# The second norm's rows in the remainder buffer of a fused attention and feed-forward kernel, with new instruction orders

## The chip, the cores and the metric

The kernel runs on one NeuronCore of a Trainium2 chip. The metric is the device time of one execution in microseconds: 1593.41 us, the median of three (1593.0 to 1603.3). The engines are TensorE (PE in the profile, its weight loads PEld), VectorE (DVE), ScalarE (ACT), GpSimd (POOL) and SyncE (SP), which issues the transfers. Each runs its own list of instructions in order; semaphores join them.

## The reference

One pre-norm block over 16 batches of 1024 rows with 256 features, all in float32:

```
xn  = layernorm(x)
Q, K, V = xn @ Wq.T + bq, xn @ Wk.T + bk, xn @ Wv.T + bv
s   = (Q @ K.T) / sqrt(256) * mask          # a Gaussian over the keys
x1  = x + softmax(s) @ V @ Wo.T + bo
x2n = layernorm(x1)
h   = gelu(x2n @ bin(w1).T + b1)            # 1024 hidden, erf gelu
out = x1 + h @ bin(w2).T + b2               # bin(w) = mean(|w|) per row * sign(w)
```

## The kernel before, in words

Every number that enters a matmul is split in two: a high part rounded to the matmul's format (names with h) and a remainder (names with l). Products take high by high, high by remainder and remainder by high. The query and key weights are folded into one matrix M, the value and output weights into one matrix N, so a batch needs *queries* (M times the normalized rows), score tiles against masked keys, a *weighing* of the normalized rows by the exponentials (weigh_rows), and a *projection* by N (project). Signs of w1 and w2 multiply in the feed-forward part; their mean sizes enter as scales.

B = 16 batches, T = 8 tiles of 128 rows, two halves of TH = 4 tiles, C = 2 chunks of 128 features, J = 8 tiles of 128 hidden features, which are computed in J hidden pairs (two tiles of hidden features for 512 rows; pairs 0 to 3 are the first half of the rows).

The order of work on each engine is written out by hand in one function batch(b, more) per engine (TensorE from L1138, VectorE from L845, ScalarE from L607, GpSimd from L431, SyncE's loop at L332). While batch b runs its second part, batch b+1 is prepared: its rows are turned and split, its queries and masked keys made, its score tiles 0 to 3 computed among the hidden pairs and output rows of b, and batch b+2's first norm is taken. TensorE's order in a steady batch b:

- score tiles 4 to 7 of b, each followed by six of the 24 steps of weigh_rows(b, 0);
- queries(b+1); project(b, 0); steps 0 to 15 of weigh_rows(b, 1);
- turn_rows_ffn(b, 0), the **first turn**: eight transposes of the second norm's rows, tiles 0 to 3;
- steps 16 to 23; hidden_pair 0; project(b, 1); hidden_pairs 1 to 3; score tile 0 of b+1;
- turn_rows_ffn(b, 1), the **second turn**, tiles 4 to 7; score tile 1;
- hidden_pairs 4 to 7; output rows 0, 1 (ffn_row); score tile 2; row 2; score tile 3; rows 3 to 7.

How the second norm's rows arise: project leaves its result in PSUM; VectorE adds it to x (add_attention, L743) and takes the statistics; GpSimd computes the root and the negated mean by pairs of tiles (root_ffn, L395 to L400); ScalarE normalizes (normalize_ffn, L519) into xn2(t); TensorE turns four tiles; ScalarE copies the high part (hi_rows_ffn, L524) and VectorE the remainder (lo_rows_ffn, L753) into rows_h and rows_l. xn2(t) lies in the last row slot of the probability buffer. The masked keys of batch b+1 lie there too (rows_t), until ScalarE has copied their high part (hi_keys, L486) and GpSimd has subtracted it (split_keys, L374). So normalize_ffn waits at tiles 0 and 4:

```
if q % TH == 0 and b < B - 1:
    act.wait_ge(kl_set, N2 * (b + 1) + q // TH + 1)
```

In the same stretch GpSimd's order is lo_probs(b, 7), root_ffn 0 and 1, both split_keys(b+1), root_attention(b+2) (L387, L389: the roots of the first norm two batches on), root_ffn 2 and 3. VectorE's is the last transpose of probabilities (turn_probs, L726), the fourth of lo_queries, invert_sums(b, 0) (L736, which waits for the sums that TensorE turns inside project(b, 0)), add_attention of four tiles, the statistics of batch b+2, lo_rows_ffn(b, 0), center_attention(b+2) (L685: waits for root_attention(b+2)), lo_outputs(b, 1) (L731: the remainder of the weighed rows; project(b, 1) needs it from its fifth matmul on), invert_sums(b, 1), add_attention of four tiles, then the splits of the gelu results (split_pair, a cast at L760 and a subtraction at L762). None of this order of GpSimd is changed in a steady batch's stretch, nor that of VectorE from add_attention(0) to split_pair 2.

regrouped_rows is a buffer that holds the first norm's rows of the next batch after a transfer between partitions. rows_l, the remainders, occupies the same memory (a placement without owner), half for half: the transposed rows of b+1 are read from it, and then their remainders are written into it. The queries of b+1 are their last reader.

Exponentials (ScalarE, L501) go to one of three slots of g; SyncE moves them in four transfers between partitions (regroup_probs, L300); VectorE transposes blocks (turn_probs), ScalarE copies the high part (hi_probs, L507), GpSimd the remainder (lo_probs, L382). Tile 7 has slot 3 of the probability buffer (p_slot), since its own is the last row that the masked keys use; its transfer waits for pv_summed, the end of the first weighing.

## Time and profile before

| | |
|---|---|
| runs | 1593.0, 1593.41, 1603.3 us |
| profiled execution | 1601.16 us, span 1599.4 us |
| mean granted clock of TensorE | 0.976 |
| TensorE busy | 1472.0 us, 92% |
| VectorE busy | 1049.8 us, 66% |
| ScalarE busy | 878.9 us, 55% |
| GpSimd busy | 975.6 us, 61% |
| chain that ended last, by engine | PE 33%, DVE 16%, ACT 15%, DMA 12%, POOL 11%, SyncE's queue 7%, issue 5% |

The span runs from the first to the last instruction. Busy shares are means over all stages; what a stage waits for is seen in the waits and timelines. "PE ps L1023 <- ACT probs L519" reads: TensorE's instruction of line 1023, which writes ps, waited for ScalarE's of line 519, which wrote probs. A timeline row gives start, duration, engine, line, what is written from what, the count of merged instructions and, in brackets, the idle time before it and what ended it. Ends of matmuls are modelled.

### The profile page before, as it was taken

To read this page: it belongs to the slowest core of one execution; us is meant where nothing else is said; L and a number is where in the kernel's file an instruction comes from. 1 tells how busy PE (TensorE), PEld (TensorE's weight loads), DVE (VectorE), ACT (ScalarE), POOL (GpSimd) and SP (SyncE) were. 2 spreads that over 40 slices of the span, in tenths; PEclk is the share of its full clock that TensorE was granted. 3 is DMA by queue.
4 is the path that set the end of the run, shared out by engine and by line. 5 is a ranking of instruction groups with operands and counts; after the bars stand their busy time and mean duration, and the time that the engine had idled before them with its cause. 6 is when DMAs were issued, how large, how long until landed. Compare 5 with 4: busy or idle time off the path is not lost.

```text
span 1599.4 us, 21090 instructions
## 1 busy us (share of the span) xinstructions
PE 1472.0 (92%) x7709; PEld 1245.5 (78%) x7709; DVE 1049.8 (66%) x1576; ACT 878.9 (55%) x1238; POOL 975.6 (61%) x1033
## 2 busy tenths in 40 slices
PE   6899999899998999999899998999999999998996
PEld 4678778787787878778787787878778777787876
DVE  7766676666776667666566766666766666764544
ACT  4655564555646455564555655556564555645432
POOL 3656747656675766647566476566747666475543
PEclk9899999999999999999999999999999999999999
DMA  5625516264270735516245261633606355260421
GB/s 185 112 66 78 134 22 122 68 95 117 44 164 4 118 93 79 132 20 115 78 82 130 37 132 44 106 105 61 151 1 119 93 79 133 32 128 26 72 61 27
DMA packets 107939, 138.50 MB, mean 87 GB/s; under 512 B 11822, under 2 KB 95164, under 8 KB 107836
## 3 DMA queue, kind: packets, MB, share of 16 engines
q1 hardware_dynamic: 107808, 137.15, 41.5%
q8 instruction: 61, 1.00, 0.3%
q14 instruction: 42, 0.34, 0.1%
q10 hardware_dynamic: 28, 0.01, 0.0%
HBM read 37.49 MB, written 16.78 MB: 34 GB/s over the span
## 4 chain that ended last, share of the span: by engine, by line
PE 33%; DVE 16%; ACT 15%; DMA 12%; POOL 11%; SPq 7%; issue 5%; ACTq 0%; DVEq 0%; POOLq 0%
PE ps L980 11%; DMA probs<-g 10%; PE ps L1044 8%; PE ps L954 7%; SPq L300 6%; ACT g L542 4%; DVE probs L726 4%; POOL rstd L397 3%; ACT probs L519 3%; POOL kl L374 3%; ACT g L501 3%; POOL probs L382 2%; POOL nmr L400 2%; DVE xin L743 2%; DVE st L747 2%
## 5 line engine op out<-in xcount | busy, mean ns | idle before, releaser
L382 POOL TENSOR_TENSOR probs<-probs 128x512 fp32r<-128x512 f32 x256 | 341.3, 1355 | 191.9 <-ACT probs L507 191.9
L980 PE MATMUL ps<-probs,xnh 128*128 128x512 f32 x1024 | 299.7, 409 | 6.2 <-ACT probs L507 6.1
L1057 PE MATMUL ps<-sgn,probs 128*128 128x256 f32 x1024 | 249.8, 284 | 11.3 <-DVE ys L770 9.7
L1058 PE MATMUL ps<-sgn,probs 128*128 128x256 f32 x1024 | 248.1, 283 | 0.0
L726 DVE STREAM_TRANSPOSE probs<-probs 128x1024 f32<-128x1024 f32 x128 | 159.2, 1243 | 134.5 <-DMA probs<-g 134.2
L507 ACT ACTIVATE probs<-probs 128x1024 fp32r<-128x1024 f32 x128 | 135.6, 1059 | 201.5 <-DVE probs L726 201.2
L980 PEld LDWEIGHTS ps<-probs,xnh 128*128 128x128 f32 x1024 | 200.3, 199 | 51.4 <-issue 9.1
L542 ACT ACTIVATE g<-ps,cols,alpha 128x512 f32<-128x512 f32 x256 | 183.1, 772 | 87.9 <-PE ps L1044 87.9
L1044 PE MATMUL ps<-rows_h,sgn 128*128 128x512 f32 x512 | 202.6, 396 | 26.5 <-DVE rows_l L753 26.5
L420 POOL TENSOR_TENSOR xin<-xin,ys 128x256 f32<-128x256 f32 x128 | 93.9, 738 | 191.7 <-DVE ys L770 191.7
L1057 PEld LDWEIGHTS ps<-sgn,probs 128*128 128x128 f32 x1024 | 195.8, 191 | 18.2 <-DVE ys L770 13.0
L1044 PE MATMUL ps<-rows_l,sgn 128*128 128x512 f32 x512 | 200.9, 392 | 0.0
L501 ACT ACTIVATE g<-ps,nmax 128x1024 f32<-128x1024 f32 x128 | 141.9, 1110 | 100.4 <-DVE nmax L718 99.8
L1058 PEld LDWEIGHTS ps<-sgn,probs 128*128 128x128 f32 x1024 | 196.1, 192 | 1.2
L718 DVE TENSOR_REDUCE nmax<-ps 128x1 f32<-128x1024 f32 x128 | 154.6, 1217 | 64.7 <-PE ps L954 64.4
L954 PE MATMUL ps<-kh,qh 128*128 128x512 f32 x512 | 164.0, 402 | 10.9 <-ACT g L501 4.8
L762 DVE TENSOR_TENSOR probs<-g,probs 128x1024 fp32r<-128x1024 f32 x128 | 163.2, 1275 | 4.4
L519 ACT ACTIVATE probs<-xin,nmr,rstd 128x256 f32<-128x256 f32 x128 | 68.4, 592 | 166.1 <-POOL nmr L400 93.6
L954 PE MATMUL ps<-kl,qh 128*128 128x512 f32 x512 | 159.6, 393 | 0.0
L980 PE MATMUL ps<-probs,xnl 128*128 128x512 f32 x512 | 158.9, 392 | 0.0
L954 PE MATMUL ps<-kh,ql 128*128 128x512 f32 x512 | 158.8, 391 | 0.0
L1044 PEld LDWEIGHTS ps<-rows_h,sgn 128*128 128x128 f32 x512 | 96.6, 189 | 56.0 <-DVE rows_l L753 33.2
(114 smaller groups left out, 2644.4 us busy)
## 6 DMA issues: line engine op xcount, KB each, us to landing
probs<-g SPq DMA_DIRECT2D x512, 128.0 KB, 3.5
xrow<-in_L_attn_x_dram SPq DMA_DIRECT2D x32, 512.0 KB, 8.3
xin<-in_L_attn_x_dram SPq DMA_DIRECT2D x32, 512.0 KB, 8.7
out_dram<-xin SPq DMA_DIRECT2D x31, 512.0 KB, 4.7
regrouped_rows<-xn SPq DMA_DIRECT2D x120, 128.0 KB, 4.6
...
```

The source lines that it names most:

```text
L382: pool.tensor_tensor(ptl(q)[:, half(n)], pt(q)[:, half(n)], pth(q)[:, half(n)].bitcast(F32), ALU.subtract).then_inc(ptl_set, 1)
L501: act.activation(exps(q).rearrange("p (i j r) -> p j i r", j=T, r=QUAD), slot(q % 2).rearrange("p h (j i r) -> p (h j) i r", j=TH, r=QUAD) ...
L507: act.activation(pth(q), pt(q), ACT.Copy).then_inc(pth_set, 1)
L542: last = act.activation(g[:, k % G_SLOTS, half(m)], ps[:, PAIR_BANK[k] + m, :], ACT.Gelu, bias=cols[:, j:j + 1], scale=alpha1[:, j:j + 1])
L718: dve.tensor_reduce(nmax[:, q:q + 1], slot(q % 2), mybir.AxisListType.XY, ALU.max, negate=True).then_inc(max_set, 1)
L726: dve.transpose(pt(q).rearrange("p (j g c) -> p g j c", j=T, c=QUAD), regrouped(q).rearrange("p (g j r) -> p g j r", j=T, r=QUAD)).then_in ...
L762: dve.tensor_tensor(hidden_part(1, n, js), val, hidden_part(0, n, js).bitcast(F32), ALU.subtract).then_inc(gl_set, 1)
L954: last = pe.matmul(ps[:, 2 * (q % 2) + n, :], part[:, c, tile(q)], keys[:, n, c, :], start=c == 0 and part is qh and keys is kh, stop=c == ...
L980: last = pe.matmul(ps[:, PV_BANK + c, :], xv[:, j, tile(c)], probs[:, lo, first:first + TH, tile(j)], start=k == 0, stop=k == len(parts) - 1)
L1044: last = pe.matmul(ps[:, PAIR_BANK[k] + m, :], sgn1[:, c, tile(j)], part[:, n, c, :], start=c == 0 and part is rows_h, stop=c == C - 1 and ...
L1057: pe.matmul(bank, probs[:, 0, r, tile(j)], sgn2[:, j, :], start=j == 0, stop=False)
L1058: last = pe.matmul(bank, probs[:, 1, r, tile(j)], sgn2[:, j, :], start=False, stop=j == J - 1)
```

## The change

The change has these parts.

1. **Second norm's rows.** xn2(t) lies in the second half of regrouped_rows; both halves of the rows use it in turn. normalize_ffn waits at tile 0 for the queries of b+1 (for the last batch, for the hidden pairs of the one before), at tile 4 for the first turn, and no longer for kl_set.
2. **ScalarE's order.** hi_keys(b+1, 1) goes behind hi_rows_ffn(b, 0); hi_outputs(b, 1) goes before the load of gelu's table; gelu pair 2 goes ahead of normalize_ffn(6, 7); hi_rows_ffn(b, 1) ahead of two pieces of hi_values; exponentials(b+1, 3) ahead of hi_probs(b+1, 1) and of the second half of normalize_attention(b+2).
3. **TensorE's order.** The second turn precedes both score tiles 0 and 1 of b+1; output rows 0 to 2 precede score tiles 2 and 3.
4. **VectorE's order.** row_max of score tile 0 precedes lo_rows_ffn(b, 1), that of tile 1 follows split_pair 3; row_max 7 precedes mask_keys(b+1, 1); invert_sums(b, 0) precedes turn_probs(b, 7); scale_outputs 0 precedes split_pair 7, scale_outputs 2 precedes row_max 2, scale_outputs 4 precedes turn_probs 2. GpSimd's lo_probs of b+1 follow output rows 2, 4 and 6.
5. **Last batch.** Tile 7 has its own slot, and its transfer waits for the batch's own kl_set; score tiles in pairs ahead of the weighing; output rows 0 and 1 in banks 0 and 1 before hidden_pairs 4 to 7.
6. **Setup.** w1 and w2 are loaded behind the rows of batch 1 and lie elsewhere; GpSimd makes the signs of w2 in three passes, VectorE only those of w1; score tiles 1 to 5 of batch 0 come before most of the turned signs; ScalarE takes exponentials 0, 1 and 2 of batch 0, with two tiles of normalize_attention(1) after each of the latter, the copy of tile 0, exponential 3, turned signs, the copy of tile 1, two more pairs of normalized tiles around exponential 4, and so comes to the copy of tile 3 and exponential 5; the eight mean sizes of w1, the turned signs of w2 and the spread of alpha2 move into batch 0, before and behind exponentials 6 and 7.

Its core (the placement of w1s, w2s and diag, the arguments b in p_slot's callers and what only moves in the setup of ScalarE and VectorE are left out; the moves above name them):

```diff
+        def p_slot(b, q):
+
+            return TH - 1 if q == T - 1 and b < B - 1 else q
+
...
         def xn2(t):
-            return probs32[:, t // TH, LAST_ROW, (t % TH) * D:(t % TH + 1) * D]
+            return regrouped_rows[:, 1, (t % TH) * D:(t % TH + 1) * D]
...
             for n in range(N2):
                 load_rows(1, n)
+            sp.dma_start(w1s[:], w1.rearrange("(j p) d -> p j d", p=P)).then_inc(w1_loaded, 16)
+            sp.dma_start(w2s[:], w2.rearrange("(c p) h -> p c h", p=P)).then_inc(w2_loaded, 16)
             sp.dma_start(bias_bc[:], bo.partition_broadcast(P)).then_inc(bcast_loaded, 16)
             sp.dma_start(b2_bc[:], b2.partition_broadcast(P)).then_inc(bcast_loaded, 16)
 
             def regroup_probs(b, q):
                 sp.wait_ge(exp_set, T * b + q + 1)
-                if q == T - 1:
+                if q == T - 1 and b < B - 1:
                     sp.wait_ge(pv_summed, N2 * b + 1)
+                elif q == T - 1:
+                    sp.wait_ge(kl_set, N2 * (b + 1))
+                if b == 0 and q == 5:
+                    sp.wait_ge(signs2_set, 1)
                 elif b > 0:
                     sp.wait_ge(ffn_summed, T * (b - 1) + q + 1)
                 for i in range(QUADS):
-                    sp.dma_start(regrouped(q)[i * QUAD:(i + 1) * QUAD, :],
+                    sp.dma_start(regrouped(b, q)[i * QUAD:(i + 1) * QUAD, :],
                                  exps(q)[:, i * (S // QUADS):(i + 1) * (S // QUADS)]).then_inc(p_back[q % QUEUED], 16)
 
...
                 regroup_rows(1, n)
+                regroup_probs(0, TH + n)
             for b in range(B):
-                for q in range(TH, T):
+                for q in range(TH if b > 0 else TH + N2, T):
                     regroup_probs(b, q)
...
+            root_attention(1)
             lo_values(0)
-            root_attention(1)
+            pool.wait_ge(w2_loaded, 16)
+            pool.tensor_scalar(sw2[:], w2s[:], 0.0, None, ALU.is_gt).then_inc(pos2_set, 1)
+            pool.wait_ge(alphas_set, C)
+            pool.wait_ge(pos2_set, 1)
+            pool.tensor_scalar(w2s[:], w2s[:], 0.0, None, ALU.is_lt).then_inc(neg2_set, 1)
+            pool.wait_ge(neg2_set, 1)
+            pool.tensor_tensor(sw2[:], sw2[:], w2s[:], ALU.subtract).then_inc(signs2_set, 1)
             lo_probs(0, 0)
             lo_probs(0, 1)
             lo_probs(0, 2)
-                    if more and r in (2, 3, 5):
-                        lo_probs(b + 1, (2, 3, 5).index(r))
+                    if more and r in (2, 4, 6):
+                        lo_probs(b + 1, r // 2 - 1)
...
-                    if q % TH == 0 and b < B - 1:
-                        act.wait_ge(kl_set, N2 * (b + 1) + q // TH + 1)
+                    if q == 0 and b < B - 1:
+                        act.wait_ge(q_summed, QG * (b + 2))
+                    elif q == 0:
+                        act.wait_ge(hidden, J * b)
+                    if q == TH:
+                        act.wait_ge(x2_turned, N2 * b + 1)
                     act.wait_ge(nmr2_set, T * b + q + 1)
                     act.activation(xn2(q), xin[s][:, q, :], ACT.Identity, bias=nmr2[:, q:q + 1],
                                    scale=rstd2[:, q:q + 1]).then_inc(xn2_set, 1)
...
@@ -633,21 +656,22 @@
                 hi_probs(b, 7)
                 if more:
                     hi_keys(b + 1, 0)
-                    hi_keys(b + 1, 1)
                 normalize_ffn(b, range(0, 4))
                 hi_rows_ffn(b, 0)
+                if more:
+                    hi_keys(b + 1, 1)
+                hi_outputs(b, 1)
                 load_table(b, ACT.Gelu)
-                hi_outputs(b, 1)
                 gelu_pairs(b, range(0, 1))
                 if more:
                     hi_values(b + 1, range(0, 2))
                 normalize_ffn(b, range(4, 6))
-                gelu_pairs(b, range(1, 2))
+                gelu_pairs(b, range(1, 3))
                 normalize_ffn(b, range(6, 8))
-                gelu_pairs(b, range(2, 4))
+                gelu_pairs(b, range(3, 4))
+                hi_rows_ffn(b, 1)
                 if more:
                     hi_values(b + 1, range(2, QG))
-                hi_rows_ffn(b, 1)
                 gelu_pairs(b, range(4, J))
                 if not more:
                     return
@@ -657,11 +681,11 @@
                 if b + 2 < B:
                     normalize_attention(b + 2, tiles_of(0))
                 exponentials(b + 1, 2)
+                hi_probs(b + 1, 0)
+                exponentials(b + 1, 3)
+                hi_probs(b + 1, 1)
                 if b + 2 < B:
                     normalize_attention(b + 2, tiles_of(1))
-                hi_probs(b + 1, 0)
...
                 turn_probs(b, 5)
+                row_max(b, 7)
                 if more:
                     mask_keys(b + 1, 1)
-                row_max(b, 7)
+                if b == 0:
+                    dve.wait_ge(alpha2_spread, 1)
+                    dve.tensor_copy(alpha2_bc[:], ps[:, QO_BANK, 0:D]).then_inc(alpha2_set, 1)
                 turn_probs(b, 6)
                 lo_outputs(b, 0)
                 if more:
                     lo_queries(b + 1, range(0, 3))
+                invert_sums(b, 0)
                 turn_probs(b, 7)
                 if more:
                     lo_queries(b + 1, range(3, QG))
-                invert_sums(b, 0)
                 for q in tiles_of(0):
                     add_attention(b, q)
...
@@ -883,27 +905,33 @@
                 split_pair(b, 0)
                 split_pair(b, 1)
                 split_pair(b, 2)
+                if not more:
+                    split_pair(b, 3)
+                    lo_rows_ffn(b, 1)
+                    scale_outputs(b, 0, more)
+                    scale_outputs(b, 1, more)
+                    for k in range(4, J):
+                        split_pair(b, k)
+                    for r in range(2, T):
+                        scale_outputs(b, r, more)
+                    return
+                row_max(b + 1, 0)
                 lo_rows_ffn(b, 1)
                 split_pair(b, 3)
-                if more:
-                    row_max(b + 1, 0)
-                    row_max(b + 1, 1)
-                for k in range(4, J):
+                row_max(b + 1, 1)
+                for k in range(4, J - 1):
                     split_pair(b, k)
-                if not more:
-                    for r in range(T):
-                        scale_outputs(b, r, more)
-                    return
                 scale_outputs(b, 0, more)
+                split_pair(b, J - 1)
                 scale_outputs(b, 1, more)
+                scale_outputs(b, 2, more)
                 row_max(b + 1, 2)
-                scale_outputs(b, 2, more)
                 turn_probs(b + 1, 0)
                 row_max(b + 1, 3)
                 turn_probs(b + 1, 1)
                 scale_outputs(b, 3, more)
+                scale_outputs(b, 4, more)
                 turn_probs(b + 1, 2)
-                scale_outputs(b, 4, more)
                 scale_outputs(b, 5, more)
                 scale_outputs(b, 6, more)
                 turn_probs(b + 1, 3)
...
             def ffn_row(b, r, more):
-                bank = ps[:, QO_BANK + r % 2 if more else PV_BANK + r % 2, 0:D]
+                bank = ps[:, (QO_BANK if more else 0) + r % 2, 0:D]
                 if r == 0:
-                    pe.wait_ge(gelu_set, J * (b + 1) - (1 if more else 0))
+                    pe.wait_ge(gelu_set, J * (b + 1) - 1 if more else J * b + 2)
                 if r % TH == 0:
                     pe.wait_ge(gl_set, J * b + (J // N2) * (r // TH + 1))
...
+            scores(0, 1)
+            scores(0, 2)
             turn_signs1(range(0, 2))
-            scores(0, 1)
             pe.wait_ge(bvb_set, C)
             for e in range(C):
                 last = pe.matmul(ps[:, 6, 0:D], bvb[:, e, :], woT[:, e, :], start=e == 0, stop=e == C - 1)
             last.then_inc(bias_summed, 1)
+            scores(0, 3)
+            scores(0, 4)
+            scores(0, 5)
             turn_signs1(range(2, 2 * C))
-            scores(0, 2)
-            pe.wait_ge(diag_set, C)
-            pe.wait_ge(nl_set, 1)
-            for c in range(C):
-                last = pe.matmul(ps[:, 7, c * P:(c + 1) * P], ones[:], diag[:, c, :], start=True, stop=True)
-            last.then_inc(alpha2_spread, 1)
-            scores(0, 3)
+
...
             def batch(b, more):
-                scores(b, TH)
                 if b == 0:
+                    weigh_rows(b, 0, range(0, 6))
                     turn_signs2(range(0, 2))
-                    scores(b, TH + 1)
+                    scores(b, 6)
+                    weigh_rows(b, 0, range(6, 12))
+                    scores(b, 7)
+                    weigh_rows(b, 0, range(12, 18))
                     turn_signs2(range(2, 4))
-                for i in range(TH):
-                    if i > (1 if b == 0 else 0):
+                    weigh_rows(b, 0, range(18, 24))
+                    spread_alpha2()
+                elif more:
+                    for i in range(TH):
                         scores(b, TH + i)
-                    weigh_rows(b, 0, range(6 * i, 6 * i + 6))
+                        weigh_rows(b, 0, range(6 * i, 6 * i + 6))
+                else:
+                    scores(b, 4)
+                    scores(b, 5)
+                    weigh_rows(b, 0, range(0, 6))
+                    scores(b, 6)
+                    scores(b, 7)
+                    weigh_rows(b, 0, range(6, 24))
                 if more:
                     queries(b + 1)
                 project(b, 0, more)
...
                 hidden_pair(b, 1)
                 hidden_pair(b, 2)
                 hidden_pair(b, 3)
-                if more:
-                    scores(b + 1, 0)
+                if not more:
+                    turn_rows_ffn(b, 1, more)
+                    for r in range(0, 2):
+                        ffn_row(b, r, more)
+                    for k in range(4, J):
+                        hidden_pair(b, k)
+                    for r in range(2, T):
+                        ffn_row(b, r, more)
+                    return
                 turn_rows_ffn(b, 1, more)
-                if more:
-                    scores(b + 1, 1)
+                scores(b + 1, 0)
+                scores(b + 1, 1)
                 for k in range(4, J):
                     hidden_pair(b, k)
-                if not more:
-                    for r in range(T):
-                        ffn_row(b, r, more)
-                    return
-                ffn_row(b, 0, more)
-                ffn_row(b, 1, more)
+                for r in range(0, 3):
+                    ffn_row(b, r, more)
                 scores(b + 1, 2)
-                ffn_row(b, 2, more)
                 scores(b + 1, 3)
                 for r in range(3, T):
                     ffn_row(b, r, more)
```

## Rows read from the trace of the kernel before

**Rows 1.** The page, busy time: us, share of the span, instructions.

```profile
PE 1472.0 (92%) x7709; PEld 1245.5 (78%) x7709; DVE 1049.8 (66%) x1576; ACT 878.9 (55%) x1238; POOL 975.6 (61%) x1033
```

**Rows 2.** Waits of TensorE: us in total, times, longest.

```profile
PE ps L1023 <- ACT probs L519: 47.6, 17, 3.1
...
PE ps L1044 <- DVE rows_l L753: 26.5, 16, 3.6
...
PE ps L1057 <- DVE ys L770: 9.7, 15, 0.9
...
PE ps L980 <- ACT probs L507: 6.1, 9, 2.0
...
PE ps L954 <- ACT g L501: 4.8, 15, 0.3
```

**Rows 3.** Timeline of TensorE, first turns: start us, us, [idle before].

```profile
99.63 1.09 PE L1023 MATMUL ps<-ident,probs 128*128 128x128 f32 x8 [2.79 <-ACT probs L519]
...
387.44 1.97 PE L1023 MATMUL ps<-ident,probs 128*128 128x128 f32 x8 [3.09 <-ACT probs L519]
...
1449.68 1.97 PE L1023 MATMUL ps<-ident,probs 128*128 128x128 f32 x8 [3.10 <-ACT probs L519]
```

**Rows 4.** Timeline of TensorE, one steady batch.

```profile
292.72 1.09 PE L1023 MATMUL ps<-ident,probs 128*128 128x128 f32 x8 [2.78 <-ACT probs L519]
...
299.37 0.40 PE L1003 MATMUL ps<-Nl,probs 128*128 128x256 f32 x2
...
299.86 0.50 PE L1003 MATMUL ps<-Nh,probs 128*128 128x256 f32 x2
...
307.82 0.39 PE L1044 MATMUL ps<-rows_l,sgn 128*128 128x512 f32 x1
...
310.89 1.09 PE L1023 MATMUL ps<-ident,probs 128*128 128x128 f32 x8
...
316.77 0.50 PE L1044 MATMUL ps<-rows_h,sgn 128*128 128x512 f32 x1 [1.54 <-DVE rows_l L753]
```

**Rows 5.** One stretch: length, busy time by engine, granted clock, DMA.

```profile
579.00:585.00 6.00, 5.96 (x25) 5.21 (x26) 1.30 (x2) 2.51 (x3) 2.49 (x3) 0.75 0.01 3
```

**Rows 6.** Timeline of GpSimd, the same batch.

```profile
287.66 5.71 POOL L374 TENSOR_TENSOR kl<-probs,kh 128x1024 fp32r<-128x1024 f32 x2
...
293.61 1.65 POOL L389 TENSOR_TENSOR rstd<-ve,mhalf 128x8 f32<-128x8 f32 x1
...
308.45 1.49 POOL L400 TENSOR_SCALAR nmr<-mv,rstd 128x1 f32<-128x1 f32 x2
```

**Rows 7.** Timeline of VectorE, the same batch.

```profile
279.63 1.24 DVE L726 STREAM_TRANSPOSE probs<-probs 128x1024 f32<-128x1024 f32 x1
...
296.05 0.16 DVE L685 SCALAR_TENSOR_TENSOR nmr<-mv,rstd 128x8 f32<-128x8 f32 x1
...
298.58 1.23 DVE L731 TENSOR_TENSOR probs<-ps,probs 128x1024 fp32r<-128x1024 f32 x1 [2.38 <-ACT probs L511]
...
308.35 1.23 DVE L762 TENSOR_TENSOR probs<-g,probs 128x1024 fp32r<-128x1024 f32 x1
```

**Rows 8.** Timeline of ScalarE, the same batch.

```profile
281.86 3.92 ACT L486 ACTIVATE kh<-probs 128x1024 fp32r<-128x1024 f32 x2
...
293.85 1.03 ACT L524 ACTIVATE rows_h<-ps 128x1024 fp32r<-128x1024 f32 x1 [1.18 <-PE ps L1023]
...
309.74 1.09 ACT L519 ACTIVATE probs<-xin,nmr,rstd 128x256 f32<-128x256 f32 x2 [2.15 <-POOL nmr L400]
```

**Rows 9.** Timeline of TensorE, in the setup and in the last batch.

```profile
57.15 1.97 PE L1134 MATMUL ps<-ident,sw 128*128 128x128 f32 x8 [6.33 <-DVE sw L777]
...
1537.09 0.70 PE L980 MATMUL ps<-probs,xnh 128*128 128x512 f32 x2 [1.96 <-ACT probs L507]
...
1568.96 0.79 PE L1044 MATMUL ps<-rows_h,sgn 128*128 128x512 f32 x1 [3.65 <-DVE rows_l L753]
```

194 lines of the change are left out of this document (101 added, 93 removed).

## The prediction

> **What bounds the kernel now.** I read the busy times first, then the waits of TensorE, then its timeline through one steady batch, then the other engines there. TensorE is busy for 92% of the span [rows 1], so only its gaps can be won. The list of its waits names them [rows 2]: 47.6 us before the turn of the second norm's rows (L1023), 16 long waits of about 2.98 us each; 26.5 us before a hidden pair (L1044), which is 1.53 us in each of 15 batches and 3.65 in the last; 9.7 us before the output rows (L1057), 6.1 us before the weighing of rows (L980) and 4.8 us before a score tile (L954).
>
> I count a batch from the start of the first turn, A. The 15 starts from 99.63 to 1449.68 are 96.43 us apart in the mean [rows 3]. From 292.72 to 387.44 it is 94.72 [rows 3, 4]. The difference is mostly the clock: after the idle 2.78 us at 292.72 eight transposes take 1.09 us, after 3.09 us at 387.44 they take 1.97; in such a stretch the granted clock was 0.75 of full, a mean over time at 2.4 GHz and at 1.2 GHz [rows 5]. The first turns that came after 3.09 and 3.10 us lost clock at once; after 2.78 and 2.79 they began at full speed [rows 3, 4]. I put the loss at 1.4 us per batch of the 1.7; the rest is scatter of small waits.
>
> **The first turn.** ScalarE writes the normalized rows into rows that the masked keys of the next batch still occupy, so it waits for both key splits of GpSimd, 5.71 us from 287.66 to 293.37 (the first suffices for the first half) [rows 6]. The rows then go to the remainder buffer, free since the queries. What is late next is the last negated mean of the first half: GpSimd ends the two small groups at 287.7, where its key split starts. invert_sums now precedes the last transpose of probabilities. That one stood at 279.63 [rows 7], before the sums were turned; it would start about 0.9 us later. Hence the copy of tile 7 is late by as much, the weighing of the second half gains a stall of about 0.5 us, and the negated means end at 288.6. The last tile, normalized by 289.2, still precedes TensorE's arrival at 290.4 (292.72 less 2.78, and 0.5): the whole wait and its clock loss go. Bounds for the new stall: 0 and 0.9.
>
> **What is put behind it.** hi_keys(b+1, 1) now comes after hi_rows_ffn(b, 0) on ScalarE, but GpSimd's queue is unchanged: second key split, then root_attention(b+2); and VectorE's queue is unchanged: lo_rows_ffn, center_attention(b+2), which waits for that root, then lo_outputs(b, 1), for which project(b, 1) waits. Before, the whole chain was over at 296.05 [rows 7]. Now it starts from A:
> - the copy of the turned rows starts 1.13 us after A and takes 1.03 [rows 4, 8];
> - one key copy, half of 3.92: 1.96 [rows 8];
> - one key split, half of 5.71: 2.86, and the root, which ends at 295.26, 1.89 us after the splits [rows 6];
> - centering, to the start of the next, 0.1; lo_outputs 1.23 [rows 7];
> - some 0.2 for the hand-offs. Sum: 10.4 us.
>
> At present the matmul that needs lo_outputs starts at 299.86, 7.14 after A, and TensorE had run out 7.05 after A (299.37 and 0.40) [rows 4]. So TensorE stands for about 3.4 us, 3.3 of them new, in the middle of project(b, 1), in the 14 batches that have a batch after the next. That is longer than the idle times after which the clock fell at once.
>
> **The second turn.** Its rows depend on a chain that starts at that same matmul: additions, statistics, roots, normalization. It ends 299.86 to 310.83, 10.97 us (309.74 and 1.09), and the turn started at 310.89 [rows 4, 8]. Now no score tile covers it: hidden_pair 3 ends at 308.21 (307.82 and 0.39), so the turn waits 2.7 us. VectorE's third gelu split now begins while GpSimd computes the last negated mean; I add 0.15 us. In exchange rows_l comes under 5.45 us of score tiles: copy after gelu 3, lo_rows_ffn after row_max, ready 6.2 us after the turn's start, needed at 6.3. The wait of 1.5 goes, just. The clock loss that follows the 3.4 us falls on matmuls before the turn. Where it delays the sums it delays the chain (about 1.0 us), where it delays only hidden pairs the 2.7 us absorb it. For a second loss after the second turn I take 0.2.
>
> **Sum for one of 14 batches.** From A to hidden_pair 4: before 24.05 (292.72 to 316.77) and 1.4 of clock, 25.45. After: 10.4 + 11.15 + 1.2 + 6.35 (transposes 0.9, two score tiles 5.45) = 29.1. That is +3.65. From there to the next A: -2.98 and 0.1 of restart; -0.4, since three output rows now precede the score tile that waits for exponentials [rows 2]; -0.4 of the 9.7/15 = 0.65 before output rows, since scale_outputs(4) goes ahead of a transpose; -0.3 before the first weighing (6.1 less 1.96, over 15), since exponentials(3) is ahead of a copy; +0.5 of above. That is -3.6 to -3.7. Net: -0.05, or -0.7 us in 14 batches. A large gain and a large cost cancel.
>
> **Batch 14** has no root or centering behind the keys: 7.14 + 11.15 + 0.2 + 6.35 = 24.85 against 25.45, and -1.1 of small waits: -1.7.
>
> **The last batch.** Two score tiles go ahead, and tile 7 has a slot of its own, so its transfer need not wait for the first weighing: the wait of 1.96 at 1537.09 goes [rows 9] with about 1.4 of clock: -3.4. At the end, 3.65 us before hidden_pair 4 [rows 9] and, since gelu has the time of two rows more, 1.5 before the first output row go; new is a wait of 2.4 us before output row 0, for gelu 3 and its split. With clock I take -4.0 (bounds -6 and -1).
>
> **The setup.** The longest wait, 6.33 us at 57.15 for w2's signs [rows 9], goes: GpSimd makes them (three passes over 2048 elements) beside scores. I followed the new order: five score tiles in a row, then the weighing waits some 5 us for the copy of tile 3, the tile whose exponential stands behind the normalization; later the turned signs wait for ScalarE after eight mean sizes. The loads of w1 and w2 go behind the next rows on SyncE's queue, and should land before their use. I take -2.5 (bounds -9 and +4: no row shows these passes on GpSimd; the nearest, a key split of 1024 elements, bounds each by 2.9 and 5.7). The first A saves its 2.79 against 0.5 of stall: -2.3.
>
> **Total:** -0.7 - 1.7 - 3.4 - 4.0 - 2.5 - 2.3 = -14.6 us. The profiled execution took 1601.2 us, 1.8 more than its span, and would take 1586.6. It lies 7.8 above the median of the runs, 1593.4; taken from that it gives **1579 us**.
>
> **Rivals.**
> 1. The centering chain is hidden. Without 3.3 us and its 1.0 of clock, 14 batches give 60 us more: 1519. For it: nothing in the rows; it would need GpSimd to finish 3 us earlier than its queue allows. 8%.
> 2. The clock is kept through the 3.4 us. Then 1.0 to 1.2 less per batch, 15 us: 1564. For it: the turn after 2.78 us kept it [rows 4]; against it: those after 3.09 and 3.10 did not [rows 3]. 17%.
> 3. Slower: the last negated mean collides with the third split. The second of two such operations ended at 309.94, when VectorE's second split was over (309.58) [rows 6, 7]. Gelu 2 is now moved ahead, so VectorE's next cast starts there. If the small operation, 0.25 us alone, is held through a cast and a subtraction, it comes 1.0 us later (1.49 for a pair instead of 0.50 is what such neighbours cost before). The second turn's wait then passes 3.1 us, and it loses clock after it as well: 1.4. That is 2.4 us in 14 batches, +34: 1613. It decides from a second-turn wait of 3.1 us. Against it: the small operations do slip in between two VectorE operations, each time. 14%.
> 4. The change doesn't do what it says, because another reader holds the buffer: queries(b+1) are its last, and these end before the first projection, and the first turn comes another two thirds of a weighing later. The wait would stay: about 1%.
>
> For the third, the trace shows a pair of small GpSimd operations at 1.49 us beside VectorE's subtraction [rows 6]. The Trainium skill, "SBUF — State Buffer", section "Who interferes with whom", says that a VectorE instruction with two SBUF inputs, or a cast in a two-port mode, holds the shared port pair for its whole length and that whoever issues first keeps it. By that rule the forecast holds if the small operation wins the gap between two instructions, and the third rival's 1613 us if it loses twice.
>
> **How the numbers follow.** Forecast 60%, own range 1568 to 1592 (setup 6, last batch 3, and 0.8 us per batch either way). With the second rival the low side is 1555; the high side, up to where the third begins, is 1605. About 2 in 10 lie outside. About 1% (16 us) is what a measurement of this kernel can tell from no change. Faster than 1577.5: a little under half of the forecast (0.28), rivals 1 and 2 (0.25), less a share of the second: 0.48. Within 1%: 0.38. Slower than 1609: 0.14, the third.
>
> **What will show it.** L1023 falls out of the first place of TensorE's waits for the first turn, but stays with 2.7 to 2.9 us for the second. L1044 before hidden_pair 4 vanishes. A new wait appears at the project's fifth matmul for lo_outputs of 3.3 us in 14 batches, with VectorE idle at centering until the root of GpSimd. The granted clock falls right behind it. The forecast is wrong if that wait is missing, or if the second turn waits over 3.1 us, or if the first turn still waits.

## The result, and the profile after

The changed kernel takes 1610.4 us (median of 14 runs, 1608.8 to 1617.9); the kernel before, beside it, 1601.0 (14 runs, 1593.0 to 1607.9). The ratio is 1.0072, with a 95% interval of 1.0050 to 1.0094. That is within 1%, but on the slow side. I had forecast 14.6 us less (1579, with a range of 1555 to 1605); it became 9.3 us more. The profiled execution took 1609.85 us with a span of 1608.1, against 1601.16 and 1599.4.

The busy times of the page and then the waits of TensorE after the change (us in total, times, longest):

```profile
PE 1471.4 (92%) x7709; PEld 1261.2 (78%) x7709; DVE 1071.1 (67%) x1574; ACT 885.5 (55%) x1238; POOL 1021.1 (63%) x1036
```

```profile
PE ps L1052 <- ACT regrouped_rows L537: 52.5, 16, 4.0
PE ps L1032 <- DVE probs L759: 47.1, 15, 3.3
PE ps L1009 <- ACT probs L521: 10.0, 19, 4.2
PE ps L1145 <- DVE bvb L842: 6.3, 1, 6.3
```

TensorE works as long as before [rows 1]. Of its waits [rows 2], those before a hidden pair (26.5 us) are gone. The wait before a turn of the normalized rows has the same sum as before, but it is now the second turn that waits, in all 16 batches, for up to 4.0 us. And 14 waits of 3.3 us in the second projection are new.

TensorE's timeline through the third batch, beside which [rows 4] are to be read:

```profile
296.55 1.04 PE L1052 MATMUL ps<-ident,regrouped_rows 128*128 128x128 f32 x8
...
306.84 0.69 PE L1032 MATMUL ps<-Nh,probs 128*128 128x256 f32 x2 [3.33 <-DVE probs L759]
...
320.12 1.52 PE L1052 MATMUL ps<-ident,regrouped_rows 128*128 128x128 f32 x8 [3.42 <-ACT regrouped_rows L537]
...
417.74 1.09 PE L1052 MATMUL ps<-ident,regrouped_rows 128*128 128x128 f32 x8 [2.96 <-ACT regrouped_rows L537]
```

The first turn (296.55) no longer waits: no bracket. The projection does (306.84), and then the second turn (320.12). The last row is the second turn of the next batch.

What the clock does behind the two waits, in stretches of that timeline (length, busy time by engine, granted clock, DMA):

```profile
306.80:311.00 4.20, 4.16 (x22) 4.16 (x23) 1.74 (x6) 0.00 (x0) 0.00 (x0) 0.59 0.01 4
311.00:316.70 5.70, 5.70 (x26) 4.40 (x25) 5.46 (x12) 3.60 (x6) 4.07 (x7) 1.00 0.00 0
...
320.10:325.00 4.90, 4.88 (x19) 4.12 (x20) 0.00 (x0) 3.37 (x5) 3.49 (x4) 0.65 0.01 2
```

TensorE is at a mean of 0.59 and 0.65 of its clock behind them (a mix of 2.4 and 1.2 GHz), and at 1.00 in between. Each stretch loses some 1.7 us (4.20 x 0.41, 4.90 x 0.35). After the wait of 2.96 the turn took 1.09 us, at full speed.

Why the second turn waits is in GpSimd's timeline of the same batch, and in VectorE's beside it:

```profile
313.85 0.55 POOL L402 TENSOR_TENSOR ve<-mv,eps 128x2 f32<-128x2 f32 x1 [0.61 <-DVE mv L777]
314.48 1.81 POOL L404 TENSOR_TENSOR rstd<-ve,mhalf 128x2 f32<-128x2 f32 x1
316.39 3.05 POOL L407 TENSOR_SCALAR nmr<-mv,rstd 128x1 f32<-128x1 f32 x2
```

```profile
313.69 0.66 DVE L788 CAST probs<-g 128x1024 fp32r<-128x1024 f32 x1
314.38 1.23 DVE L790 TENSOR_TENSOR probs<-g,probs 128x1024 fp32r<-128x1024 f32 x1
315.56 0.69 DVE L788 CAST probs<-g 128x1024 fp32r<-128x1024 f32 x1
316.29 1.23 DVE L790 TENSOR_TENSOR probs<-g,probs 128x1024 fp32r<-128x1024 f32 x1
317.43 0.69 DVE L788 CAST probs<-g 128x1024 fp32r<-128x1024 f32 x1
318.15 1.24 DVE L790 TENSOR_TENSOR probs<-g,probs 128x1024 fp32r<-128x1024 f32 x1
```

The last two negated means took 3.05 us, where the pair took 1.49 before [rows 6]. They ended only when VectorE's third split was over (319.39), which before had not begun by then. The last normalization follows at 319.47. Read link by link, the addition ends at 314.40, the root at 316.29 and the first negated mean at 318.17, each within 0.05 us of the end of a cast (314.35, 316.25, 318.12), and the second negated mean ends at 319.44 with the last subtraction. Between a subtraction and the cast behind it nothing slipped in: the root and the first negated mean stood through both. Two microseconds earlier, beside VectorE's additions and statistics, the root of tiles 4 and 5 took 0.70 us (at 311.94) and their pair 0.50 (at 312.74). So it is casts and subtractions that come with the long times, not any work of VectorE.

**Where the time went.** A is again the start of a first turn. The starts that the sums need:

```profile
101.93 1.03 PE L1052 MATMUL ps<-ident,regrouped_rows 128*128 128x128 f32 x8
...
1464.19 1.04 PE L1052 MATMUL ps<-ident,regrouped_rows 128*128 128x128 f32 x8
...
1555.15 1.03 PE L1052 MATMUL ps<-ident,regrouped_rows 128*128 128x128 f32 x8
```

| stage | before | after | measured | forecast |
|---|---|---|---|---|
| start to first A | 99.63 | 101.93 | +2.3 | -2.5 - 2.3 = -4.8 |
| A to A, mean of 14 | 96.43 | 97.30 | +0.87, x14 = +12.2 | -0.05, x14 = -0.7 |
| batch 14, A to A | 96.40 | 90.96 | -5.4 | -1.7 - 3.4 = -5.1 |
| last A to the end | 53.3 | 52.9 | -0.4 | -4.0 |
| span | 1599.4 | 1608.1 | +8.7 | -14.6 |

The batch of 97.30 divides at hidden pair 4: A to there took 30.55 in the mean of 14 batches (25.34 before; I had 29.1 and 25.45), and from there to the next A 66.76 (71.09 before; I had about 67.4). So the error of a steady batch lies ahead of hidden pair 4: +1.45 there, -0.6 behind it.

The setup, TensorE first, then VectorE and GpSimd:

```profile
45.75 2.08 PE L1145 MATMUL ps<-woT,bvb 128*128 128x256 f32 x4 [6.28 <-DVE bvb L842]
...
62.74 1.19 PE L1009 MATMUL ps<-probs,xnh 128*128 128x512 f32 x2 [4.20 <-ACT probs L521]
```

```profile
39.02 6.68 DVE L842 TENSOR_SCALAR bvb<-ones,cols 128x128 f32<-128x128 f32 x2
```

```profile
40.23 5.38 POOL L435 TENSOR_SCALAR sw<-w2s 128x2048 f32<-128x2048 f32 x1
45.78 5.37 POOL L438 TENSOR_SCALAR w2s<-w2s 128x2048 f32<-128x2048 f32 x1 [0.17 <-POOL sw L435]
51.23 4.63 POOL L440 TENSOR_TENSOR sw<-sw,w2s 128x2048 f32<-128x2048 f32 x1
```

The wait of 6.33 us for w2's signs [rows 9] is gone, and one of 6.28 for a tile of 128 x 128 (bvb, the value bias spread over a tile, which TensorE multiplies by the output weights) stands in its place: VectorE's second bvb operation ended when GpSimd's first pass did. I had no row for these passes; each took 4.6 to 5.4 us.

Not all of the later first A is the change's. The first score tile started at 28.40 us for 26.85, since the first product of the weights ran slow, 3.38 us for 1.97. That comes with either setup: a run with the old one (below) has 3.48, one with the new one 1.97. So 1.5 us of the +2.3 are scatter.

### The profile page after: what moved, and what is told of

It is laid out like the page before. It is cut to its first block, busy times and chain, and to the rows that moved or that the text cites. A ratio compares the mean times of both kernels' runs of the same rounds, so it can differ in the third digit from the quotient of the medians.

```text
span 1608.1 us, 21094 instructions
## 1 busy us (share of the span) xinstructions
PE 1471.4 (92%) x7709; PEld 1261.2 (78%) x7709; DVE 1071.1 (67%) x1574; ACT 885.5 (55%) x1238; POOL 1021.1 (63%) x1036
## 4 chain that ended last, share of the span: by engine, by line
PE 68%; POOL 10%; DVE 8%; ACT 6%; DMA 3%; issue 2%; SPq 2%; DVEq 0%; POOLq 0%; ACTq 0%
PE ps L983 19%; PE ps L1009 18%; PE ps L1073 7%; PE ps L1086 5%; PE ps L1087 5%; PE ps L1032 4%; POOL nmr L407 3%; POOL kl L381 3%; DMA probs<-g 3%; PE ps L1052 2%; SPq L306 2%; ACT kh L500 2%; POOL rstd L404 2%; PE ps L963 2%; PE ps L966 2%
## 5 line engine op out<-in xcount | busy, mean ns | idle before, releaser
L1009 PE MATMUL ps<-probs,xnh 128*128 128x512 f32 x1024 | 286.2, 394 | 10.0 <-ACT probs L521 10.0
L1009 PEld LDWEIGHTS ps<-probs,xnh 128*128 128x128 f32 x1024 | 190.3, 189 | 51.7 <-issue 13.8
L427 POOL TENSOR_TENSOR xin<-xin,ys 128x256 f32<-128x256 f32 x128 | 98.7, 776 | 166.7 <-DVE ys L798 166.3
L537 ACT ACTIVATE regrouped_rows<-xin,nmr,rstd 128x256 f32<-128x256 f32 x128 | 71.8, 596 | 171.0 <-POOL nmr L407 171.0
L1032 PE MATMUL ps<-Nh,probs 128*128 128x256 f32 x512 | 110.8, 326 | 48.4 <-DVE probs L759 47.1
```

The lines of the kernel that those rows point to most:

```text
L1009: last = pe.matmul(ps[:, PV_BANK + c, :], xv[:, j, tile(c)], probs[:, lo, first:first + TH, tile(j)], start=k == 0, stop=k == len(parts) - 1)
L1032: last = pe.matmul(bank, part[:, c, tile(at)], N[:, c, :], start=k == 0 and c == 0, stop=k == 2 and c == C - 1)
```

## The experiments

My theory after reading this: three costs, each of which can be lifted by moving a line or two. **C**, the wait in the projection for the root that stands behind the second key split. **H**, the hold: GpSimd's small operations stand still while VectorE splits gelu outputs, which lengthens the second turn's wait and brings a loss of clock behind it. **S**, the setup's new collisions. The rival to H was that the second turn's wait costs nothing beyond what it hides, or that its small operations are slow of themselves; the rival to all was that another engine stands right behind, so that nothing adds up. The kernel before, run beside each group of experiments, had medians of 1598.8 to 1601.1 us, so differences of 1 or 2 us between groups say nothing.

### Root between the key splits

```
     split_keys(b + 1, 0)
-    split_keys(b + 1, 1)
     root_attention(b + 2)
+    split_keys(b + 1, 1)
```

> The changed kernel (1610 us) with one line moved: on GpSimd the root of the batch after the next (root_attention(b+2)) now stands between the two key splits instead of behind them. Theory (the two stalls and the clock behind them are the cost): the wait of 3.3 us in project(b, 1) for lo_outputs falls to 0.1 to 0.5 us (it is then set by the copy of the outputs, which stands on ScalarE behind a key copy), the second turn of the normalized rows still waits 3.0 to 3.4 us because its chain starts at that same matmul, and with the first stall gone the matmuls behind it run at full clock: 14 x (3.0 + 1.3) = 60, so about 1550 us. Rival A (the clock is lost through the second turn's wait alone): only 14 x 3.0 = 42, 1568 us. Rival B (another link of the same chain is as late as the root was, for instance the second key split or the outputs' copy): the wait stays over 2 us and the time over 1590.

Measured: 1576.4 us (1574.3 to 1579.1), ratio 0.9845 (0.9822 to 0.9868). C is gone from the list of waits, as expected, but the gain is 34 us and not 60. The second turn of one batch:

```profile
405.00 1.97 PE L1053 MATMUL ps<-ident,regrouped_rows 128*128 128x128 f32 x8 [3.98 <-ACT regrouped_rows L538]
```

With the first wait gone, the matmuls behind it run at full clock and TensorE reaches the second turn sooner, while the small operations of the chain to it are held as long as before (3.05 us here too): the wait grew to 3.98 us, and in 12 of the 14 batches the turn behind it ran at half speed or close to it. In the mean of 14 batches 3.9 us are gained from A to the second turn and 1.4 lost again between it and hidden pair 4.

### Score tile 0 ahead of the second turn, alone and with the root

```
+    scores(b + 1, 0)
     turn_rows_ffn(b, 1, more)
-    scores(b + 1, 0)
     scores(b + 1, 1)
```

> The changed kernel with TensorE's order alone changed: score tile 0 of the next batch stands ahead of the turn of the normalized rows' second half again, tile 1 stays behind it. Theory: the second turn's wait falls from 3.2 to 0.5 us (one tile of 2.72 us covers it), the wait of hidden pair 4 for the turned rows' remainders comes back with 0.1 to 0.5 us only (ScalarE is free earlier than in the kernel before), and the clock loss behind the turn goes: 14 x (2.5 + 1.0) = 49, about 1561 us. Rival: hidden pair 4 waits 1.5 us again as in the kernel before, 14 x (1.2 + 0.7) = 27, about 1583. If the second turn's wait cost nothing beyond what it hides: no change, 1610.

Measured: 1560.6 us (1557.2 to 1561.6), ratio 0.9738 (0.9712 to 0.9764). The sum of waits before turns fell from 52.5 us to 11.1, and hidden pair 4 doesn't wait: one tile ahead of the turn and one behind it cover both. The second turn ran at full clock in 15 of 16 batches.

Both diffs together:

> Both edits together: root between the key splits and score tile 0 ahead of the second turn. Theory (both stalls are independent costs, and below them nothing is near): the sum of the two gains, 60 + 49 = 109 us, about 1501 us. Rival: another engine's chain is next within a few us per batch (exponentials, gelu, GpSimd's additions), so that the gains are not additive: 1530 to 1545.

Measured: 1503.1 us (1499.8 to 1503.2), ratio 0.9381 (0.9359 to 0.9403). The second turn of one batch, and a stretch of one batch's length (columns as above, the clock third from the end):

```profile
391.85 1.09 PE L1053 MATMUL ps<-ident,regrouped_rows 128*128 128x128 f32 x8 [1.28 <-ACT regrouped_rows L538]
```

```profile
372.40:462.60 90.20, 88.00 (x477) 75.72 (x476) 68.92 (x103) 54.94 (x76) 64.37 (x65) 1.00 0.43 94
```

The clock is 1.00 over the batch, and no other engine stood right behind. The gains don't merely add up: 34 and 50 alone, 107 together. Each wait that stayed still cost its clock. Behind C in the score tile run, and behind the second turn, whose wait had grown to 3.97, in the root run:

```profile
301.60:305.80 4.20, 4.15 (x22) 4.15 (x23) 1.71 (x6) 0.00 (x0) 0.00 (x0) 0.59 0.01 4
```

```profile
309.80:314.80 5.00, 4.91 (x16) 4.24 (x17) 0.00 (x0) 3.43 (x6) 3.14 (x4) 0.50 0.01 2
```

### The hold, lifted in part: gelu of pair 2 back

```
-    gelu_pairs(b, range(1, 3))
+    gelu_pairs(b, range(1, 2))
     normalize_ffn(b, range(6, 8))
-    gelu_pairs(b, range(3, 4))
+    gelu_pairs(b, range(2, 4))
```

> The changed kernel with ScalarE's gelu of pair 2 behind the last two normalizations again, as in the kernel before, so that VectorE's third split cannot start while GpSimd computes the last roots and negated means. Theory (third rival of the prediction: these small GpSimd operations are held by VectorE's split; one root took 1.81 us and the last two negated means 3.05 us where 0.70 and 0.50 are usual): the last negated mean comes 0.3 to 1.0 us sooner, the second turn's wait falls from 3.2 to 2.2 to 2.9 us, with less clock lost behind it: 14 x (0.5 + 0.3) = 11, about 1599 us. Rival (the first two splits alone hold them, the third does not matter): 1610, wait unchanged.

Measured: 1584.1 us (1581.6 to 1585.6), ratio 0.9891 (0.9871 to 0.9911): 26 us less, more than the 11 I expected. GpSimd in one batch:

```profile
404.10 1.77 POOL L404 TENSOR_TENSOR rstd<-ve,mhalf 128x2 f32<-128x2 f32 x1
405.97 1.49 POOL L407 TENSOR_SCALAR nmr<-mv,rstd 128x1 f32<-128x1 f32 x2
```

The pair is back at 1.49 us, as before the change [rows 6], since VectorE's third split comes later: the first of the two is still held, the second is not. The second turn's wait is 1.2 to 2.1 us and the clock stays up behind it. This one move of the change, gelu 2 ahead of two normalizations, is worth more than the whole difference between the two kernels.

### The hold, lifted whole: VectorE waits

```
+    dve.wait_ge(nmr2_set, T * (b + 1))
     split_pair(b, 0)
```

> The changed kernel (1610 us) with one wait added: VectorE does not begin its gelu splits of the first half (split_pair(b, 0)) until GpSimd's eight negated means of the second norm are written. All orders stay. Theory (the third rival of the prediction: the last root and negated means are held while VectorE's splits run, 1.81 and 3.05 us for 0.70 and 0.50): VectorE waits 1.5 us, the roots take their usual 0.2 + 0.7 + 0.5 us, the last normalization runs right behind gelu of pair 2, and the second turn's wait falls from 3.2 to about 1.3 us, short enough that the clock stays up: 14 x (1.9 + 1.3) = 45, about 1565 us (the gelu-order run gave 1584). Rival (the small operations are slow for another reason, such as GpSimd's own start-up): root and negated means stay long, VectorE only loses its 1.5 us, 1610 to 1630 us.

Measured: 1586.3 us (1584.4 to 1588.4), ratio 0.9909 (0.9881 to 0.9938). GpSimd, then VectorE:

```profile
310.97 0.70 POOL L404 TENSOR_TENSOR rstd<-ve,mhalf 128x2 f32<-128x2 f32 x1
311.78 0.50 POOL L407 TENSOR_SCALAR nmr<-mv,rstd 128x1 f32<-128x1 f32 x2
312.23 2.97 POOL L376 TENSOR_TENSOR xnl<-xn,xnh 128x512 fp32r<-128x512 f32 x2
```

```profile
312.31 1.76 DVE L788 CAST probs<-g 128x1024 fp32r<-128x1024 f32 x1 [1.69 <-POOL nmr L407]
314.10 2.18 DVE L790 TENSOR_TENSOR probs<-g,probs 128x1024 fp32r<-128x1024 f32 x1
```

With nothing else changed but VectorE's idleness the small operations take 0.70 and 0.50 us instead of 1.81 and 3.05. So H is shown: they are held by VectorE's splits and not slow of themselves. But the hold works both ways. VectorE starts 1.7 us late, right beside GpSimd's next operation, and its cast and subtraction take 3.94 us instead of 1.89. Hidden pair 4 then waits 1.0 to 1.3 us for the remainders (rows_l) that stand behind the splits in VectorE's queue. That is why I expected 1565 and got 1586: I had counted the 1.5 us of idleness, not where it would end.

The added wait with the root's diff and that of gelu 2:

> Root between the key splits, VectorE's wait for the negated means, and gelu of pair 2 behind the last two normalizations; both score tiles stay behind the second turn as in the change. Theory: both stalls are gone without moving a score tile: the wait in project(b, 1) is 0, the last row is normalized 0.1 to 0.5 us ahead of TensorE's arrival, the second turn's wait is 0 to 0.3 us: the 1503 us of the root and score run less 14 x 1.28 = 18, about 1485 us. Rival: the splits that now start 1.5 us later make the first output row or hidden pair 4 wait (gelu 3 and row_max 0 stand in the same queues): 1490 to 1510.

Measured: 1538.9 us (1536.9 to 1540.1), ratio 0.9611 (0.9584 to 0.9639).

The added wait with the root's and the score tile's diffs:

> Root between the key splits, score tile 0 ahead of the second turn, VectorE's wait for the negated means; gelu's order as in the change. Theory: the tile covers what the gelu of pair 2 still costs, the second turn's wait goes from 1.28 us to 0: 1503 - 18 = 1485 us, the same as the run without the score tile moved. Rival: row_max of tile 0, now behind splits that start later, or the copy of the turned rows becomes late for hidden pair 4, which has one tile of cover only: 1490 to 1500.

Measured: 1551.9 us (1544.0 to 1556.8), ratio 0.9677 (0.9641 to 0.9714). Both rivals came, and harder. The waits of TensorE, of the first and of the second:

```profile
PE ps L1075 <- DVE rows_l L782: 35.3, 15, 2.4
```

```profile
PE ps L1075 <- DVE rows_l L782: 45.3, 15, 3.0
```

The second turn waits 0.4 us or not at all, hidden pair 4 instead 2.35 or 3.02, and in the second run the stretch behind it is longer too (68.56 us from hidden pair 4 to the next A, 66.80 without the wait). The second is the run without the added wait (1503) plus this wait: 49 us of harm from one semaphore.

### Root, score tile and gelu 2

Three of the diffs above, without the added wait:

> Root between the key splits, score tile 0 ahead of the second turn (1503 us together, with 1.28 us of wait left before that turn) and gelu of pair 2 behind the last two normalizations. No wait is added to VectorE, since the run with one showed that its splits then meet GpSimd's next operation and take twice as long. Theory: with gelu 2 moved back one of the two negated means escapes the third split (1.49 us for the pair instead of 3.05), the last row is normalized ahead of TensorE's arrival, and rows_l still comes 0.1 us in time for hidden pair 4: 1503 less 14 x 1.3 = 18, about 1485 us. Rival (what happened with the added wait: hidden pair 4 waits for rows_l instead): 1495 to 1510.

Measured: 1515.4 us (1511.8 to 1517.5), ratio 0.9472 (0.9449 to 0.9494). The rival: the second turn no longer waits, but

```profile
305.90 0.50 PE L1074 MATMUL ps<-rows_h,sgn 128*128 128x512 f32 x1 [1.31 <-DVE rows_l L782]
```

The third split, now later, and row_max of score tile 0 stand ahead of rows_l on VectorE. The wait is as long as the one removed, and score tile 1 waits 0.24 more. In the mean of 14 batches the stretch up to the second turn became 1.3 us shorter than in the root and score run, that from it to hidden pair 4 became 2.0 longer (5.65 for 3.69).

### The remainders first

On top of the run above, with bvb early and invert_sums back (both below):

```
-    gelu_pairs(b, range(2, 4))
+    gelu_pairs(b, range(2, 3))
     hi_rows_ffn(b, 1)
+    gelu_pairs(b, range(3, 4))
...
-    row_max(b + 1, 0)
     lo_rows_ffn(b, 1)
+    row_max(b + 1, 0)
```

> The combination of 1501 us, in which hidden pair 4 waits 1.31 us for the remainders of the turned rows and nothing else waits for long, with two lines moved: ScalarE copies the turned rows ahead of gelu of pair 3, and VectorE makes their remainders ahead of row_max of score tile 0. Theory: the copy ends at 1.2 us behind the turn, the remainders 1.2 to 1.5 us later, behind the third split, and the wait falls from 1.31 to 0.2 us: 1501 - 14 x 1.2 = 1484 us. Rival (gelu of pair 3, now 1 us later, or row_max becomes what hidden pair 4 or score tile 2 waits for): 1490 to 1501.

Measured: 1483.4 us (1480.6 to 1484.9), ratio 0.9282 (0.9261 to 0.9304). It is the fastest version found, 7.2% below the kernel before. The same wait, and a stretch of one batch's length:

```profile
384.89 0.50 PE L1075 MATMUL ps<-rows_h,sgn 128*128 128x512 f32 x1 [0.18 <-DVE rows_l L783]
```

```profile
384.80:473.90 89.10, 88.38 (x477) 75.71 (x478) 66.59 (x99) 54.86 (x77) 63.46 (x65) 1.00 0.44 95
```

TensorE is busy for 88.4 of 89.1 us at full clock. What is left is the amount of its work.

### The small terms and the setup

bvb moved forward on VectorE:

```
 lo_queries(0, range(0, QG))
+dve.wait_ge(consts_set, 5)
+for c in range(C): dve.tensor_scalar(bvb[:, c, :], ...)
 stats_attention(1, range(T))
...
 center_attention(1)
-dve.wait_ge(consts_set, 5)
-for c in range(C): dve.tensor_scalar(bvb[:, c, :], ...)
```

> The changed kernel with VectorE's two bvb operations (128 x 128) right behind lo_queries(0, ...) as in the kernel before, ahead of the statistics, instead of beside GpSimd's three passes over w2. Theory (a second case of operations of VectorE and GpSimd that hold each other: the two took 6.68 us beside a GpSimd pass of 5.38): they take 1 to 3 us, TensorE's wait of 6.28 us before the matmul that reads bvb goes, of which 1 us comes back before score tile 3; the copies of tiles 2 and 3 come sooner too, so that the 4.2 us before the first weighing shrink: -4 to -8 us, about 1604 us. Rival (the passes over w2 end as late as before and set the end of the setup, through lo_probs on GpSimd and the turned signs): the saved wait comes back there, 1608 to 1610.

Measured: 1607.1 us (1604.6 to 1614.0), ratio 1.0047 (1.0028 to 1.0067), 3 us less than the change, with the intervals overlapping. The stage tells more. VectorE, then TensorE:

```profile
27.15 1.76 DVE L832 TENSOR_SCALAR bvb<-ones,cols 128x128 f32<-128x128 f32 x2
```

```profile
55.81 1.19 PE L1009 MATMUL ps<-probs,xnh 128*128 128x512 f32 x2 [5.14 <-ACT probs L521]
...
75.29 1.61 PE L1169 MATMUL ps<-ident,sw 128*128 128x128 f32 x8 [3.37 <-ACT sgn L627]
```

The two operations took 1.76 us for 6.68, and the 6.28 us of wait fell to 0.34. Of these 5.9, 0.9 came back before the weighing and 2.9 before the turned signs, which wait for ScalarE behind the eight mean sizes. That leaves 2.1; the first turned sums (the sums of the exponentials, which TensorE turns inside project(b, 0)) came 3.6 us sooner, 88.09 for 91.69. Theory and rival were each half right.

This, and on top of the root, score tile and gelu 2:

```
-    invert_sums(b, 0)
     turn_probs(b, 7)
     lo_queries(b + 1, range(3, QG))
+    invert_sums(b, 0)
```

> The kernel above with two more edits: bvb right behind lo_queries(0, ...) (3 us less when alone) and invert_sums(b, 0) behind turn_probs(b, 7) again, as before the change. Theory: the stall of 0.33 us at the weighing of the second half goes in 15 batches (5 us), and the first half's negated means, 0.9 us later, still precede the first turn: 1485 - 3 - 5 = 1477 us. Rival (the first turn now waits for them, 0.3 to 0.9 us): 1482 to 1490.

Measured: 1501.2 us (1497.4 to 1504.0), ratio 0.9384 (0.9361 to 0.9406), 14 us less than without the two edits, where I expected 8. The stall before the second weighing, 0.33 us in 15 batches, is gone, and between the two turned sums of a batch 17.07 us pass instead of 17.64: the place of invert_sums was worth 0.57 us per batch, not 0.33, since the first matmuls after a stall are longer too. The rest is the setup (first turned sums 5.9 us sooner, 84.73 for 90.59).

The same two edits on the root and score run:

> The root and score run (1503 us) with bvb early and invert_sums(b, 0) behind turn_probs(b, 7), gelu's order as in the change. Theory: both edits are worth the same here as beside gelu's other order, where they took 14 us (6.5 us up to the first batch and 0.6 us per batch: the stall of 0.33 us and the slower matmul start behind it): 1503 - 14 = 1489 us, with 1.3 us of wait left before the second turn. Rival (the first half's negated means, now 0.9 us later, push the key splits and with them the second turn): 1493 to 1500.

Measured: 1489.9 us (1488.7 to 1491.3), ratio 0.9322 (0.9300 to 0.9345). As expected: the two edits add up on another base.

The setup as in the kernel before, behind it the change (some lines of many):

```
-pool.tensor_scalar(sw2[:], w2s[:], 0.0, None, ALU.is_gt)
...
+negatives(sw2, w2s)
+signs(1, sw2, w2s)
...
-scores(0, 1)
-scores(0, 2)
 turn_signs1(range(0, 2))
+scores(0, 1)
```

> The steady batches and the last batch as in the change (1610 us), the setup and the first batch's own orders as in the kernel before: signs of w2 on VectorE, the loads of w1 and w2 early, turned signs between the score tiles. Theory (the prediction's setup term of -2.5 had the wrong sign; from the two traces the new setup costs about 5 us more than the old one up to the first batch's queries): about 1605 us, first queries of batch 1 some 4 us sooner than in the change. Rival (the prediction's term was right and the loss is chance of the clock at the start): 1611 to 1613.

Measured: 1614.3 us (1608.7 to 1621.4), ratio 1.0094 (1.0068 to 1.0121). The total doesn't show the gain: the first A came at 98.66 us instead of 101.93, 3.3 sooner, but the batches were 0.6 us longer each, with the two long waits and the clock's answer to them.

The same with the root's and the score tile's diffs:

> The setup and the first batch's own orders as in the kernel before, on the base of the root and score run (1503 us), whose steady batches have no wait long enough to lower the clock. Theory: the setup's cost is read here without the scatter of the steady batches; in the two traces with the long waits the old setup reached the first projection 3.1 us sooner but the batches behind it were 0.7 us longer each, which is put down to those waits and the clock, not to the setup: 1503 - 3 = 1500 us. Rival (the batches behind the old setup are longer for a reason of their own, such as later loads): 1507 to 1512.

Measured: 1497.1 us (1496.0 to 1499.1), ratio 0.9371 (0.9351 to 0.9391), 6 us less than with the new setup by the medians, though the intervals of the two ratios overlap. The batches are as long as with the new setup. The first turned sums come at 85.44 us instead of 92.83; 2.3 of these 7.4 are there already at the first score tile (26.85 for 29.12), with the first product of the weights at 1.97 us for 3.34, which the change doesn't touch, so about 5.1 are the setup's. The two pairs of traces thus put the new setup at 3 to 5 us more than the old one. The longer batches behind it were not its doing.

## Why the prediction was wrong

**C was right.** I had 3.4 us, 3.3 of them new; it is 3.3, in 14 batches. The chain from A to lo_outputs' reader was 10.4 us forecast and 10.29 measured (296.55 to 306.84). The clock fell right behind it (0.59), so rival 2 is out. The wait of the first turn vanished, as did that of hidden pair 4, and the stall before the second weighing came as 0.33 us in the bounds 0 and 0.9.

**The step that failed** is "I add 0.15 us" for VectorE's third gelu split beside the last negated means, and with it "for a second loss after the second turn I take 0.2". This is rival 3, to which I gave 14%. I had priced it at 1.0 us later and 2.4 us per batch. The pair became 1.56 us longer (3.05 for 1.49), the second turn waited 3.2 us in the mean of the 14 batches instead of 2.7, and in 6 of them the turn itself ran slow. The stretch from the second turn to hidden pair 4 took 7.21 us in the mean for my 6.35, and that from the late matmul of the projection to the second turn 13.1 for my 12.35 (11.15 and 1.2). With the hold lifted A to hidden pair 4 took 28.67 (gelu run) and 28.74 (added wait), for my 29.1. So the order of the sum was sound, and the hold alone is worth 24 to 26 us: without it the change would have come out at 1584 to 1586, which is 17 and 15 us below the kernel before that ran beside it, for the 14.6 forecast. That this agrees so well is in part luck. In the gelu run a steady batch took 95.44 us for the 96.38 of my sum, 13 us less in 14 batches, and the setup and the last batch took 10 of these back.

That 1610 lies near the 1613 of rival 3 is luck as well: the hold is worth 24 to 26 us and not 34, and setup and last batch brought 10.7 us that the rival didn't have. Its sign, a second-turn wait of over 3.1 us, rested on first turns after 3.09 and 3.10 us that ran slow. The same trace has one after 3.08 (at 1161.06) that took 1.09 us and one after 2.79 (at 1257.58) that took 1.82, so no such limit could be read from it, nor that the clock would hold after 2.7.

The prediction named the row that decides it. The Trainium skill, "SBUF — State Buffer", section "Who interferes with whom", says of VectorE's two-port modes that whoever issues first keeps the shared port pair for its whole instruction and the other is blocked, and of an instruction with two inputs in SBUF that it contends with GpSimd's reads. The traces agree in both directions: 0.50 became 3.05 on GpSimd, and 1.89 became 3.94 on VectorE; and a subtraction held as a cast did. I had argued against the rival that "the small operations do slip in between two VectorE operations, each time". They do, but only where a cast ends and its subtraction has yet to begin; one that starts just behind that point stands until the next. The four links took 0.2, 0.7 and 0.5 us (the last for two) without the hold and 0.55, 1.81 and 3.05 with it, 4.0 us more, which is about one VectorE instruction for each. The kernel before already showed that price, in the 1.49 and in its root, which takes 0.70 in the run with the added wait:

```profile
306.55 1.81 POOL L397 TENSOR_TENSOR rstd<-ve,mhalf 128x2 f32<-128x2 f32 x1
```

I read it as a fixed offset of the chain, where it was a rate that one more split would raise.

**The setup** had the wrong sign: -2.5 forecast, +3 to +5 measured. I followed the new orders by queue and by wait and found the 5 us before the weighing (4.2 measured), but took bvb at its own length. It is the same kind of collision, with GpSimd's long passes: 6.28 us of wait in place of the 6.33 removed. My bounds of -9 and +4 did cover most of it. No run isolates which move of the setup costs the rest.

**The small terms of a steady batch** (output rows, scale_outputs, exponentials(3)) stand in the stretch behind hidden pair 4, which came 0.6 us shorter than forecast. No run takes them apart.

**The last batch.** Its first part came as forecast with batch 14 (-5.4 for -5.1), but by luck of two errors: A to hidden pair 4 took 27.40 us for 24.85, with a second-turn wait of 3.98, and the rest was shorter than forecast by more. The second part, -4.0 forecast, was -0.4. The second turn there waits 3.99 us, also for held negated means, and two output rows now follow it. The row by itself is the same turn in the kernel before:

```profile
1574.54 1.97 PE L1052 MATMUL ps<-ident,regrouped_rows 128*128 128x128 f32 x8 [3.99 <-ACT regrouped_rows L537]
1577.94 0.55 PE L1086 MATMUL ps<-sgn,probs 128*128 128x256 f32 x1 [1.44 <-DVE probs L790]
```

```profile
1564.12 1.19 PE L1023 MATMUL ps<-ident,probs 128*128 128x128 f32 x8 [2.63 <-ACT probs L519]
```

The waits of 3.65 [rows 9] and of 1.54 before the first output row are gone, the turn waits 1.36 more, and 1.44 is new: -2.4 together, where my waits made -2.75 (-3.65, -1.5 and +2.4). So the waits were nearly right and the clock was not: it stood at 0.50 over the 7.5 us from that turn on, while I had counted on 1.25 us of gain from it. No run isolates this part.

**Sum of the errors**: setup and first A +7.1, steady batches +12.9, batch 14 -0.3, end +3.6, together 23.3, which is the distance of +8.7 from -14.6. Of the 7.1, 1.5 are the scatter of the first product.

**The sizes of my later expectations** failed for two reasons. Where VectorE got the added wait, the hold came back on its side. In the others, a wait of 3 to 4 us costs itself and, behind it, often 1.7 to 2.5 us of clock (0.59 over 4.2 us, 0.50 over 5.0 us); taking one away changes the length of the other. Gains of two such waits were 34 and 50 apart and 107 together.
